# Graph kernel with four gather hops on one core: one compare writes a round's eight one-hot tiles in hops 3 and 4

## What is computed

```
h = x;  for _ in range(2):                       # layer 0: hops 1 and 2, rows of 256
    h = 0.5 * segment_sum(norm[:, None] * h[src], dst) + 0.5 * x
...
h = (1 + eps1) * x + segment_sum(x[src], dst)    # layer 1: hop 3, rows of 256
h = relu(relu(h @ W1a + b1a) @ W1b + b1b)
h = (1 + eps2) * h + segment_sum(h[src], dst)    # layer 1: hop 4, rows of 512
```

## Time and profile before

| what | us |
|---|---|
| median of three runs | 3348.63 |
| lowest and highest of them | 3346.47, 3349.78 |
| span of the profiled execution, first to last instruction | 3723.0 |
| POOL busy in it, of which gathers (L385, x1664) | 1607.3, 1590.4 |
| PE busy; DVE busy; ACT busy | 2861.5; 1157.5; 437.7 |
| one-hot tiles of all hops (L489, x1696) on DVE | 457.7 |

### The profile page before, as it was taken

One profiled execution on the slowest core, in us unless ns is written; L12 is line 12 of the kernel. 1 busy time (PEld: TensorE's weight loads), 2 busy tenths in 40 slices (PEclk: granted clock), 3 DMA queues, 4 the chain that ended last, 5 costly groups with the idle time before them and its releaser, 6 DMA issues. The chain is left out here.

```text
span 3723.0 us, 40053 instructions
## 1 busy us (share of the span) xinstructions
PE 2861.5 (77%) x13236; PEld 2189.1 (59%) x13236; DVE 1157.5 (31%) x3469; ACT 437.7 (12%) x933; POOL 1607.3 (43%) x1694
## 2 busy tenths in 40 slices
PE   5566666767777777896666766987777778999999
PEld 3455544556565665685555655557676776656666
DVE  7733333342222225245233322212222222122212
ACT  0211101010000001332110001220000000142232
POOL 0266666646666661103666666116666664000000
PEclk9988899876666667898877777899889989998999
DMA  2133333333333331003332233036566564000001
GB/s 84 56 87 89 86 90 87 89 99 89 90 90 90 90 90 30 26 1 105 89 88 85 83 88 89 27 105 174 166 173 171 170 174 117 0 18 9 17 9 35
DMA packets 117895, 312.31 MB, mean 84 GB/s; under 512 B 28061, under 2 KB 45461, under 8 KB 117385
## 3 DMA queue, kind: packets, MB, share of 16 engines
q0 software_dynamic: 94048, 275.10, 25.9%
q1 hardware_dynamic: 23721, 35.49, 2.8%
HBM read 290.90 MB, written 19.58 MB: 83 GB/s over the span
## 5 line engine op out<-in xcount | busy, mean ns | idle before, releaser
L385 POOL DMA_INDIRECT rows<-table,cur x1664 | 1590.4, 956 | 1406.8 <-issue 636.5
L399 PE MATMUL ps<-onehot,rows 128*128 128x128 f32 x8320 | 1579.3, 339 | 695.3 <-DMA rows<-table,cur 518.9
L399 PEld LDWEIGHTS ps<-onehot,rows 128*128 128x128 f32 x8320 | 1348.9, 238 | 1020.6 <-issue 771.8
L501 DVE TENSOR_TENSOR AS<-AS,ps 128x256 f32 (+1 forms) x208 | 101.7, 489 | 1764.7 <-PE ps L399 1585.8
L489 DVE TENSOR_SCALAR onehot<-iota_w,rel,wgt 128x128 f32<-128x128 f32 x1696 | 457.7, 360 | 8.1 <-DVE iota_w L522 3.3
L832 PE MATMUL ps<-AS,WA 128*128 128x400 f32 (+1 forms) x768 | 255.2, 494 | 3.3 <-DVEq L1490 1.8
L832 PE MATMUL ps<-NN,WA 128*128 128x400 f32 (+1 forms) x640 | 214.3, 495 | 0.0
L832 PEld LDWEIGHTS ps<-AS,WA 128*128 128x128 f32 x768 | 146.6, 191 | 110.4 <-issue 3.8
L832 PEld LDWEIGHTS ps<-NN,WA 128*128 128x128 f32 x640 | 121.8, 191 | 87.1 <-issue 1.6
L1035 ACT ACTIVATE AS<-ps,small 128x400 f32<-128x400 f32 (+1 forms) x224 | 131.2, 586 | 336.8 <-PE ps L832 336.8
L1550 DVE SCALAR_TENSOR_TENSOR X<-ps,WA,X 128x256 f32<-128x256 f32 x150 | 72.6, 484 | 272.3 <-PE ps L901 272.3
(11 more groups left out here) (267 smaller groups left out, 1597.2 us busy)
## 6 DMA issues: line engine op xcount, KB each, us to landing
rows<-table,cur POOLq DMA_INDIRECT x1664, 3.7
table<-NN SPq DMA_DIRECT2D x10, 640.0 KB, 3.9
table<-rows SPq DMA_DIRECT2D x6, 1024.0 KB, 4.2
WA<-in_experts SPq DMA_DIRECT2D x6, 768.0 KB, 4.4
X<-in_x SPq DMA_DIRECT2D x1, 3072.0 KB
out<-X SPq DMA_DIRECT2D x4, 640.0 KB
table<-AS SPq DMA_DIRECT2D x1, 1920.0 KB, 7.3
table<-AS SPq DMA_DIRECT2D x1, 1280.0 KB, 8.4
```

The costliest lines, as they stand in the source:

```text
L385: nc.gpsimd.indirect_dma_start(rows[:, k, 0:hop_width(h) * P], None, table[h - 1][:, :], bass.IndirectOffsetOnAxis(cur[:, j * U + k:j * U ...
L399: mm = nc.tensor.matmul(EDGE[j][:, c * P:(c + 1) * P], rows[:, k, c * P:(c + 1) * P], onehot[:, j * U + k, :], start=(k == 0 and c == 0), ...
L501: nc.vector.tensor_tensor(win, win, EDGE[j][:, 0:nch * P].rearrange("p (c n) -> p c n", n=P), ALU.add).then_inc(added[h], 1)
```

## The change

In `one_hots`, for hops 3 and 4, one DVE instruction compares the column numbers (repeated eight times) with the eight columns of `rel` (each spread over 128 columns) and writes all eight tiles; it waits once, for the eighth product that used the buffer, and raises the semaphore by eight. The multiplication by `wgt` is gone there. So that padded edges still give nothing, their entry of `rel` becomes -1, a number that no column has: the last column of `rel` is replaced by (rel + 1) x mask - 1 in the set-up, and the fill of `wgt` with 1 is dropped. Hops 1 and 2 are as they were.

```diff
@@ -481,6 +481,14 @@
             nch = hop_width(h)
 
             def one_hots(row, buffer, r=None):
+                if h >= 3:
+
+                    if r is not None:
+                        dve.wait_ge(product_done[h], r * U + U)
+                    nc.vector.tensor_tensor(
+                        onehot[:, buffer * U:(buffer + 1) * U, :], iota_w[:, :].unsqueeze(1).to_broadcast([P, U, P]),
+                        rel[:, bass.ds(row * U, U)].unsqueeze(2).to_broadcast([P, U, P]), ALU.is_equal).then_inc(onehot_ready[h], U)
+                    return
                 for k in range(U):
                     c = row * U + k
                     if r is not None:
@@ -1475,8 +1483,10 @@
                     X[:, g * GROUP:(g + 1) * GROUP, :], X[:, g * GROUP:(g + 1) * GROUP, :], N[:, g * GROUP:(g + 1) * GROUP, :], ALU.add))
 
 
-            st.add(nc.vector.memset(wgt[:, 0:C - 1], 1.0))
-            st.add(nc.vector.tensor_scalar(wgt[:, C - 1:C], iota_p, float(EDGES - (C - 1) * P), None, ALU.is_lt))
+            st.do(nc.vector.tensor_scalar(wgt[:, C - 1:C], iota_p, float(EDGES - (C - 1) * P), None, ALU.is_lt))
+            st.do(nc.vector.scalar_tensor_tensor(out=rel[:, C - 1:C], in0=rel[:, C - 1:C], scalar=1.0, in1=wgt[:, C - 1:C],
+                                                 op0=ALU.add, op1=ALU.mult))
+            st.add(nc.vector.tensor_scalar(rel[:, C - 1:C], rel[:, C - 1:C], 1.0, None, ALU.subtract))
             st.add(nc.vector.memset(AT[:, :, NP:WIDE], 0.0))
 
             st.add(nc.vector.memset(AT[:, HC - 1, NODES:NP], 0.0))
```

## The result

| kernel | median us | runs | against before |
|---|---|---|---|
| before | 3347.55 | 4, 3346.13 to 3349.78 | |
| changed | 3390.39 | 4, 3387.1 to 3399.24 | 1.0125, 95% interval 1.0108 to 1.0142 |

The account below looks back on a forecast made before the run. POOL, writing gathers 1.25 us apart, was taken to set the pace, with DVE, PE and transfers having slack. Terms -1 + 31 + 23 = +53 us on a median of 3348.6 gave 3402 us; range 3345 to 3455 us.

Parts of the forecast that it names:

- the 374 us: Kernel before: profiled span 3723.0 us over median 3348.63 us; said to be the recorder's, as POOL's 355 us of product waits.
- The hold and its formula: First gather starting inside a compare is delayed by compare's end minus gather's start minus 0.13 us; earlier-started gathers lose nothing.
- Hop 4: 31 us forecast: Hop 4: each compare hits the fifth gather, 0.51 or 0.72 us, taken as 0.6; over 52 rounds 31 us.
- Hop 3: 23 us forecast: Hop 3: compare spread evenly over a gather's period, 0.48 us, taken as 0.45; over 52 rounds 23 us.
- The stretch under the old tiles: Hops 3 and 4: few gathers stretched beside the eight short instructions, now removed; -1 us.
- signs of being right: One 1.22 us compare and one 1.4 to 2.0 us gather a round; hop 4 mean over 1020 ns; hops 1, 2 unchanged.
- the earlier row numbers: Gathers' column numbers ready 0.9 us earlier: nothing. Rival: hop 3's first 25 rounds gain 23 us, 3326 us; chance 0.06.
- the later first tile: Hops 3 and 4: PE can use a round's first tile 0.9 us later; used many us later.
- the single wait: Wait moved to the front, for the previous round's last product; the add just ahead already waited for it: costs nothing.
- the set-up: In front of hop 3: one memset fewer, two column instructions and two settled waits more; 0, between -0.4 and +0.6 us.
- A swallowed stall: Rival: POOL really waits for products in ordinary runs, so a late fifth gather shortens that wait; 3348 to 3354 us, chance 0.14.
- Less time locked: Rival: all DVE time in these instructions holds POOL; 2.14 us a round becomes 1.22, 96 us gained, 3253 us; chance 0.04.

Follow-up runs that it names:

- the second profile: The kernel before, with no edit, profiled once more: 3344.77 us, with a span of 3342.7 us.
- the PSUM kernel: The changed kernel, but in hop 4 the compare reads the column numbers from a free PSUM bank: 3363.94 us, ratio 1.0055 to the kernel before.

## Why the prediction was right, and what in it was not

**What bounds the kernel: right, for a wrong reason.** The conclusion, that POOL issues gather after gather and sets the pace, is what the second profile shows: 1.25 us from start to start, 10.0 us a round. The argument was that the recorder makes up the 374 us. The experiment denies it: two executions under the profiler, one of each kernel, have spans of 3342.7 and 3387.8 us beside medians of 3347.55 and 3390.39. The profiled execution of the earlier trace rows was an odd one: none of the 27 runs of the kernel before is above 3355.32 us. In it POOL waited about 2.5 us in almost every round of hop 4 for the fourth tile's product (POOL waits once for each half of a round, for the last product of that half). PE's timeline there, the fourth and fifth tiles:

```profile
2577.74 2.22 PE L399 MATMUL ps<-onehot,rows 128*128 128x128 f32 x16 [0.23 <-issue]
```

The first eight of these matmuls, the fourth product, end near 2578.9; POOL's next gather starts at 2582.26, 3.4 us later. So the product was there and POOL learned of it late. Why stays open. The step from rows to pace was partly luck: it called the waits for products no part of an ordinary run, which is so, but by a cause that is not there, and it came out because the waits of that execution summed to about what was missing.

**The hold and its formula: right.** In the changed kernel the held gathers end 0.81 to 0.82 us after the compare, where the earlier trace rows gave 0.82 and 0.83. With the measured starts and ends the formula gives the length of all 51 held gathers of hop 4 to 0.01 us. Its other half, that a gather which starts with or before the instruction is not held, is right too, and reaches further than the account behind it. If a gather needed something only 0.13 us in, a compare that starts less than 0.13 us after the gather would hold it. The changed kernel has five such compares, and six more that start up to 0.01 us before a gather, and none of these gathers is held. What a gather does in its first 0.13 us was not tried. Hop 3 after has a case, on DVE and on POOL:

```profile
1672.81 1.26 DVE L488 TENSOR_TENSOR onehot<-iota_w,rel 128x1024 f32<-128x1024 f32 x1
```

```profile
1671.48 1.03 POOL L385 DMA_INDIRECT rows<-table,cur  x1 [0.30 <-issue]
1672.81 0.95 POOL L385 DMA_INDIRECT rows<-table,cur  x1 [0.30 <-issue]
1674.06 0.94 POOL L385 DMA_INDIRECT rows<-table,cur  x1 [0.30 <-issue]
```

The gather that starts at the same moment takes 0.95 us; the compare takes 0.04 us longer; the next gather starts at its end and is free. The 1.03 us of the gather before has a cause of its own, a short instruction of two SBUF operands that DVE runs at its start.

**The terms.** The compare: 1.22 us taken, 1222 ns measured. Hop 4: 31 us forecast; gathers there have a mean of 1014 ns after and 949 in the second profile, and POOL's work is 26.6 us more. I had taken 0.6 us of delay a round from 0.51 and 0.72; 28 us in 52 rounds is 0.54. Hop 3: 23 us forecast, 20.1 measured. Spreading the delay evenly came out, because its rounds do fall on both sides: the rows above show a free one, and the largest delay by a compare is 1.04 us. On DVE and on POOL:

```profile
1842.69 1.23 DVE L488 TENSOR_TENSOR onehot<-iota_w,rel 128x1024 f32<-128x1024 f32 x1
```

```profile
1842.75 1.99 POOL L385 DMA_INDIRECT rows<-table,cur  x1 [0.30 <-issue]
```

The stretch under the old tiles was taken as 1 us from the execution of 3723.0 us, where gathers often stood waiting and perhaps met fewer tiles (not shown); in the second profile hop 4's mean is 949 and not 947, 1.2 us in that hop alone. Forecast +53, measured +42.8 on the medians: direction and mechanism right, the size 10 us, or a quarter, too high, spread over both hops. Some 4 us of that is not in POOL's rows at all: these say 46.7 us, the medians 42.8, and single runs scatter by as much. Two of the signs of being right were missed by a little: the mean of hop 4's gathers rose to 1014 ns and not to over 1020, and some held gathers are shorter than 1.4 us, the one of 1.38 us above among them.

**What costs nothing, as forecast:** the earlier row numbers, the later first tile and the single wait (the PSUM kernel has all three and pays nothing in hop 4), the set-up (0.9995).

**The rivals.** A swallowed stall is out: the pauses after a held gather stay 0.30 us. Earlier row numbers: the changed kernel's list of POOL's waits (us in total, times, longest) has for them only the usual pause:

```profile
POOL rows L385 <- DVE cur L504: 3.0, 10, 0.3
```

Less time locked is out: the second profile has hop 4's gathers at 942 to 1033 ns under the old tiles, so there was next to nothing to gain.

The Trainium skill, in SBUF — State Buffer, "SBUF: two separate sides", says that whoever starts first keeps the shared port pair for the whole instruction; by it a compare that begins inside a gather would wait for the gather. The compares of hop 4 deny it, by line, in ns min/median/max:

```profile
L488 DVE TENSOR_TENSOR onehot<-iota_w,rel x51: 1217/1220/1227, 2258.5 to 2787.8; 128x1024 f32<-128x1024 f32 x51
```

All 51 last 1217 to 1227 ns, though nearly all begin inside a gather. The measurement decides: a long compare holds a gather up by as much as 1.04 us, and no compare of 1.22 us in any run lasts more than 1.30 us.

## What to carry to other kernels

When GpSimd issues indirect DMAs one after another and sets the pace, count a DVE instruction by its length and by where its operands lie. Here one compare of 1.22 us with two SBUF operands cost 43 us in 104 rounds; the eight short ones, or the same compare with an operand in PSUM, cost next to nothing. Merging small instructions to relieve an engine that has time to spare can thus make a kernel slower. And where a profiled execution is far from the runs beside it, profile once more before explaining the difference.

## What was not expected of the hardware

Two things. One execution of the kernel before took 3723.0 us by its span, 11% over the others of that kernel, and POOL learned of finished products microseconds late in nearly every round of hop 4; why was not found. And among several compares in a row two gathers were held for longer than one compare lasts: 0.58 us beside compares of 0.42 us, and 0.95 us beside compares of 0.69 us.
